# Two heads share a strip's weights in float32, and a final addition and a normalisation move behind the next maxima

## The chip, the cores and the metric

The kernel runs on one core of one Trainium2 chip. The metric is the time of one execution on the device in microseconds, as the median of several runs.

## The reference

Sixteen sequences of 256 tokens with 128 features go through three stages: `x += 0.5 * ffn(ln(x))`, `x += attn(ln(x))`, `x += 0.5 * ffn(ln(x))`. All is float32. `ffn` is a whole transformer block, `attn` a dilated attention whose queries, keys and values are the rows themselves.

```python
def ffn(x):                                  # 16 heads of 8 features, 8 experts, 2 chosen
    q, k, v = split(x @ w_qkv)
    scores = q @ k.T / sqrt(8)               # causal, 256 x 256 for each head
    h = layernorm(x + softmax(scores) @ v @ w_o) * g1 + b1
    w = two largest of softmax(h @ wg), normalised
    moe = sum over chosen e: w[e] * (gelu(h @ w1[e] + bb1[e]) @ w2[e] + bb2[e])
    return layernorm(h + moe) * g2 + b2
def attn(x):                                 # rate 4, segments of 64, so 4 interleaved sequences of 64
    return softmax(x @ x.T / sqrt(128)) @ x / 4
```

## The kernel before, in words

**Order.** A chunk is two sequences (512 tokens); eight chunks go through two passes of `ffn`, which makes 16 jobs `m`. The attention of one sequence is `n` (32 in all), and takes two *halves* of time. `make_order` (L53) writes one list by hand: for each half 17 slots (`SLOTS`, L48) in a fixed order, into which pieces of many stages are put. A half has `scores_0`, `first_c`, `turn_tiles`, `second_a`, `misc_1`, `exps_0`, `weigh_last`, `second_b`, `scores_1`, `misc_2`, `second_c`, `exps_1`, `weigh_0`, `first_a`, `misc_3`, `first_b`, `end`. Every engine walks through this one list and issues its own part of each piece, in this order, with semaphores between the engines. So an engine that waits in one piece holds back all its later pieces.

**Memory between the engines.** PSUM has eight banks: `ps_quad` of four, which scores and exponentials use in turn, in two pairs `a` (`pair_full`, `pair_free`), and `ps_ring` of four, which all other pieces take round robin (`take`, `full`, `freed`): a piece needs the bank that the piece four places earlier left.

**Attention of a job.** `norm`, `norm_apply`: layer norm on VectorE, with the power -0.5 on GpSimd (`powers`, L975). `turn`, `project` (L383): rows are transposed, queries and keys projected into `qk`, features on the partitions. `spread` (L312, SP's queue) writes `qk` to DRAM and reads it back with four DMAs so that heads lie in strips of 32 partitions: strip `i` of `q4` and `k4` holds, for group `j` of four, the 8 features of head `4j + i` at rows 4 to 11, and in rows 0 to 3 of `k4` constants (-1 in row `j`).
`scores(n, j)` (L398) does four heads, one in each strip: for each of the four a matmul over 256 keys for the later 128 queries (L409) and one over 128 keys for the earlier (L413), both with 32 rows and 128 columns of weights, then four full-array bf16 matmuls that add the causal mask (L417). VectorE takes row maxima over each pair of banks (L748), which frees the pair. After the fourth group `shift` transposes the maxima (L427), and VectorE adds them to the queries' unused rows (`q4s`, L765), so that the next product has them subtracted. `exps(n, j)` (L431) computes the scores again, keys as weights, per strip 128 queries (L439) and 256 queries (L443); ScalarE takes the exponential (L618), GpSimd zeroes what is above the diagonal (L972). `weigh` (L447) multiplies with the values, in column strips of 32. `rows`, `merge`, `attn_out` bring the result back. A float32 matmul stands in the profile as two instructions (two passes, each with its weight load).

**Behind it.** `mid_norm` and `mid_norm_apply` (L787, L791; L710 is the line of `normalise`, L1001 and L1004 are GpSimd's scale and offset), `turn_mid`, `route`, `gate`; per set of two jobs `rank` and `scatter` (rows sorted by expert, indirect DMAs L1017); 23 tiles in 8 batches through `turn_tiles`, `first` (L537), `second` (L546, whose output VectorE takes at L877), with a weight load from DRAM for each; `gather` (L1030), `combine`, `end_norm`, `end_norm_apply` (GpSimd's L1037) and `end_add` (VectorE's L910), which waits for L1037. `mid_norm_apply` and `end_add` stand in the slot `end`, directly ahead of the next half's `scores_0`. Between the passes the dilated attention `long_*` runs.

**Start.** VectorE fills `values`, `q4` and `k4` ahead of its first statistics; TensorE turns the bias (L583) once all small inputs and constants are there.

Of the kernel before, what the change touches and what calls it, by code (L numbers as in the profile page):

```python
# [25 lines left out]
SLOT = 32  # L26

# [22 lines left out]
FIRST_HALF, LAST_HALF = -9, HALVES + 25  # L50


def make_order():  # L53
# [18 lines left out]
    for m in range(JOBS):  # L72
        first = 4 * m
        put(first - 5, "misc_2", ("norm", m))
        put(first - 5, "misc_3", ("norm_apply", m))
        put(first - 4, "misc_1", ("turn", m))
        put(first - 4, "misc_2", ("project", m, 1))
        put(first - 4, "second_c", ("spread", m, 1))
        put(first - 4, "misc_3", ("project", m, 0))
        put(first - 4, "end", ("spread", m, 0))  # L80
        put(first - 1, "misc_1", ("values", m))
        put(first + 1, "misc_3", ("residual", m))
        put(first + 5, "misc_1", ("merge", m))
        put(first + 5, "misc_2", ("attn_out", m))
        put(first + 5, "misc_3", ("mid_norm", m))
        put(first + 5, "end", ("mid_norm_apply", m))
        put(first + 6, "misc_2", ("turn_mid", m))
        put(first + 6, "misc_3", ("route", m))
        put(first + 7, "misc_1", ("gate", m))

    for s in range(SETS):
# [17 lines left out]
        for c in range(2):  # L109
# [6 lines left out]
            put(first + 24 + c, "end", ("end_add", m))  # L116
            if m >= CHUNKS:
                put(first + 24 + c, "end", ("store", m - CHUNKS))
            else:
# [7 lines left out]
                put(half + 1, "end", ("long_values", m, 1))  # L127
    return [p for half in range(FIRST_HALF, LAST_HALF + 1) for slot in SLOTS for p in at[half, slot]]
# [10 lines left out]
def build(nc, x, w_qkv, w_o, g1, b1, wg, w1, bb1, w2, bb2, g2, b2, out):  # L139
# [8 lines left out]
    with ExitStack() as ctx:  # L148
# [9 lines left out]
        wqkv, wo, wgate = sb("wqkv", [P, 3 * D]), sb("wo", [P, D]), sb("wgate", [P, E])  # L158
        bb1_rows, bb1_t = sb("bb1_rows", [E * FC, P]), sb("bb1_t", [P, E * FC])
        g1_row, b1_row = sb("g1_row", [P, D]), sb("b1_row", [P, D])  # L160
        g2_row, b2_row = sb("g2_row", [P, D]), sb("b2_row", [P, D])
# [3 lines left out]
        row_of = sb("row_of", [P, SLOT])  # L165
# [3 lines left out]
        zeros = sb("zeros", [P, D])  # L169
# [5 lines left out]
        q4, k4 = sb("q4", [P, 2, GROUPS, TOK]), sb("k4", [P, 2, GROUPS, TOK])  # L175
        q4s = sb("q4s", [P, 2, GROUPS, S])
        values = sb("values", [P, 2, TT, HEADS, SLOT])
        probs = sb("probs", [P, PROBS, 4, 3 * P])
        part_max = sb("part_max", [P, 3, 4, GROUPS])
# [24 lines left out]
        weights = sb("weights", [P, WEIGHTS, ROW])  # L204
        act = sb("act", [P, ACTS, FC, P])
# [12 lines left out]
        small_in, x_in = sem("small_in"), sems("x_in", CHUNKS)  # L218
        const_dve, const_pool = sem("const_dve"), sem("const_pool")
# [9 lines left out]
        shift_ready, selected = sem("shift_ready"), sem("selected")  # L229
# [50 lines left out]
        CONSTANTS_DVE = 3  # L280
# [4 lines left out]
        def _(sp):  # L285
            sp.dma_start(xs[:, 0:TT, :], x_tiles[0]).then_inc(x_in[0], 16)
            sp.dma_start(wqkv[:, :], w_qkv).then_inc(small_in, 16)
            sp.dma_start(wo[:, :], w_o).then_inc(small_in, 16)
            sp.dma_start(wgate[:, :], wg).then_inc(small_in, 16)
            sp.dma_start(bb1_rows[:, :], bb1.rearrange("e (c p) -> (e c) p", p=P)).then_inc(small_in, 16)  # L290
            for row, given in ((g1_row, g1), (b1_row, b1), (g2_row, g2), (b2_row, b2)):
# [5 lines left out]
            def pack():  # L297
# [10 lines left out]
                for i in range(2):  # L308
                    sp.dma_start(sorted_h[i].rearrange("(t p) d -> p t d", p=P),
                                 zeros[:, :].unsqueeze(1).broadcast_to([P, TILES, D])).then_inc(zeroed, 16)  # L310

            def spread(m, which):  # L312
                rows = parts[m % 2, which]
                into = (q4, k4)[which]
                freed(sp, ("project", m, which))
                sp.dma_start(rows, qk[:, which, :]).then_inc(parts_out[which], 16)
                if m >= 2:
                    if which:
                        pair_used(sp, ("exps", 2 * m - 3, GROUPS - 1), 1)
                    else:  # L320
                        freed(sp, ("shift", 2 * m - 3))
                elif m == 0 and which:
                    sp.wait_ge(const_dve, CONSTANTS_DVE)
                    sp.wait_ge(const_pool, CONSTANTS_POOL)
                sp.wait_ge(parts_out[which], 16 * (m + 1))
                of_head = rows.rearrange("(j i d) t -> i d j t", j=GROUPS, i=4)
                for i in range(4):
                    sp.dma_start(into[32 * i + 4:32 * i + 4 + HD, m % 2, :, :], of_head[i]
                                 ).then_inc(parts_in[which][m % 2], 16)
# [12 lines left out]
            def load_weights(s, t):  # L342
                if t == 0:
                    sp.wait_ge(places_ready, s + 1)
                if (s, t) == (0, 0):
                    sp.wait_ge(packed_in, 16 * PACKED)
                k = tile_no(s, t)
# [13 lines left out]
            def store(c):  # L361
# [3 lines left out]
            pieces = {"spread": spread, "load_tiles": load_tiles, "load_weights": load_weights,  # L365
                      "store_tiles": store_tiles, "store": store}
            for kind, *at in ORDER:
                if kind in pieces:
                    pieces[kind](*at)
                if (kind, *at) == ("spread", 1, 0):  # L370
# [4 lines left out]
        def _(pe):  # L375
            def turn(m):
# [6 lines left out]
            def project(m, which):  # L383
# [3 lines left out]
                pe.matmul(bank(use), wqkv[:, which * D:(which + 1) * D], xn_t[:, :], start=True, stop=True  # L387
                          ).then_inc(ring_full, 1)

            def project_values(m):  # L390
                use = ("values", m)
                take(pe, use)
                for tt in range(TT):
                    mm = pe.matmul(bank(use)[:, tt * P:(tt + 1) * P], xn_t[:, tt * P:(tt + 1) * P],
                                   wqkv[:, 2 * D:3 * D], start=True, stop=True)
                mm.then_inc(ring_full, 1)

            def scores(n, j):  # L398
                m, at, par = n // 2, n % 2 * S, n // 2 % 2
                if j == 0 and n % 2 == 0:  # L400
                    for which in range(2):
                        pe.wait_ge(parts_in[which][par], 64 * (m // 2 + 1))
# [12 lines left out]
                for a in range(2):  # L415
                    for i in (2 * a, 2 * a + 1):
                        mm = pe.matmul(ps_quad[:, i, P:3 * P], ident_bf[:, :],  # L417
                                       causal[:, :].unsqueeze(1).broadcast_to([P, 2, P]), start=False, stop=True,
                                       skip_group_check=True)
# [11 lines left out]
            def exps(n, j):  # L431
                at, par = n % 2 * S, n // 2 % 2
                if j == 0:
                    freed(pe, ("shift", n))
                for a in range(2):
                    pe.wait_ge(pair_free[a], QUAD_NO["exps", n, j])
                    for i in (2 * a, 2 * a + 1):
                        rows = slice(32 * i, 32 * i + SLOT)
                        pe.matmul(ps_quad[:, i, 0:P], k4[rows, par, j, at + P:at + S], q4s[rows, n % 2, j, P:S],  # L439
                                  start=True, stop=True, tile_position=(32 * i, 0))  # L440
# [660 lines left out]
```

## Time and profile before

| | us |
|---|---|
| median of 3 runs | 1308.93 |
| lowest, highest | 1301.49, 1309.05 |
| the profiled execution | 1304.4 |
| its span, first to last instruction | 1302.6 |
| mean granted TensorE clock in it | 0.908 |

The profile is of one execution. The span is what views of the trace cover; 1.8 us of the execution lie outside it. "Idle before" is the time in which an engine had nothing running before an instruction, and the name behind it is what released it. The clock is given as a share of 2.4 GHz.

### The profile page before, as it was taken

The numbers are of one execution on the slowest core, as the hardware profiler recorded it, in microseconds if no ns is written. First come the engines' busy times: TensorE is split into PE (matmuls) and PEld (weight loads), VectorE is DVE, ScalarE is ACT, GpSimd is POOL, SyncE is SP. The second block draws the span as 40 slices with busy tenths as digits, with TensorE's granted clock in tenths as the row PEclk, the third lists the DMA queues.
The fourth block names the chain that finished last, engine by engine and source line by source line (L and its number), as shares of the span: only waits on it lengthen the run. The fifth ranks groups of instructions, "written<-read, shape, count | busy, mean of one in ns | idle before, by whom it ended". The sixth has DMA issues, their size and how long they took to land. (4 is left out here: it accounts for less than half of the span.)

```text
span 1302.6 us, 29447 instructions
## 1 busy us (share of the span) xinstructions
PE 1084.2 (83%) x11041; PEld 865.4 (66%) x11041; DVE 682.6 (52%) x2097; ACT 640.7 (49%) x1377; POOL 569.0 (44%) x708
## 2 busy tenths in 40 slices
PE   1788988899988898989989799988989799877570
PEld 0555655677776776867777577767777677776570
DVE  4445555545456664576555664566546654350313
ACT  0033333465656555645656466555546556633340
POOL 1023237222645446444645436454545436635505
PEclk8598888898989999989989899889989889988795
DMA  5085012463555435444545435363454445567661
GB/s 111 3 169 136 10 25 64 149 174 128 160 161 147 137 122 167 151 120 129 150 150 153 128 120 161 121 177 116 122 160 149 132 135 194 174 212 263 209 225 44
DMA packets 116467, 180.98 MB, mean 139 GB/s; under 512 B 12360, under 2 KB 79464, under 8 KB 116328
## 3 DMA queue, kind: packets, MB, share of 16 engines
q1 hardware_dynamic: 108136, 162.32, 43.2%
q0 software_dynamic: 8192, 16.79, 4.2%
q8 instruction: 89, 1.46, 0.5%
q14 instruction: 50, 0.41, 0.1%
HBM read 145.10 MB, written 38.68 MB: 141 GB/s over the span
## 5 line engine op out<-in xcount | busy, mean ns | idle before, releaser
L748 DVE TENSOR_REDUCE part_max<-ps_quad 128x6 f32<-128x768 f32 x256 | 233.1, 952 | 155.9 <-PE ps_quad L417 155.9
L618 ACT ACTIVATE probs<-ps_quad 128x768 f32<-128x768 f32 x256 | 196.0, 809 | 231.4 <-PE ps_quad L443 230.9
L972 POOL TENSOR_SCALAR_AFFINE_SELECT probs<-probs 128x512 f32<-128x512 f32 x256 | 162.2, 644 | 266.0 <-ACT probs L618 261.7
L654 ACT ACTIVATE act<-ps_ring,weights 128x128 f32<-128x128 f32 x736 | 205.3, 378 | 116.4 <-PE ps_ring L537 115.6
L537 PE MATMUL ps_ring<-tile_t,weights 128*128 128x128 f32 x1472 | 207.8, 288 | 23.1 <-DVE tile_y L877 12.9
L546 PE MATMUL ps_ring<-weights,act 128*128 128x128 f32 x1472 | 213.2, 294 | 9.0 <-DVE tile_y L877 5.4
L537 PEld LDWEIGHTS ps_ring<-tile_t,weights 128*128 128x128 f32 x1472 | 186.6, 199 | 39.8 <-issue 36.7
L546 PEld LDWEIGHTS ps_ring<-weights,act 128*128 128x128 f32 x1472 | 191.6, 204 | 30.0 <-issue 19.0
L977 POOL TENSOR_TENSOR rstd<-var_eps,power 128x4 f32<-128x4 f32 x56 | 57.9, 1034 | 275.4 <-DVE var_eps L704 275.4
L439 PE MATMUL ps_quad<-q4s,k 32*128 32x128 f32 x1024 | 100.5, 337 | 68.2 <-DVE part_max L748 68.2
L1030 POOL DMA_INDIRECT picked<-sorted_outputs,place x128 | 123.6, 966 | 76.5 <-issue 76.5
L877 DVE TENSOR_TENSOR tile_y<-ps_ring,weights 128x128 f32<-128x128 f32 x184 | 52.7, 287 | 187.8 <-PE ps_ring L546 187.6
L1017 POOL DMA_INDIRECT sorted_rows<-h_rows,place x128 | 124.3, 971 | 56.3 <-issue 33.9
L409 PE MATMUL ps_quad<-k,q 32*128 32x256 f32 x1024 | 123.2, 482 | 26.3 <-DMA q<-query_key_parts 21.3
L439 PEld LDWEIGHTS ps_quad<-q4s,k 32*128 32x128 f32 x1024 | 63.6, 194 | 104.5 <-issue 55.0
L443 PE MATMUL ps_quad<-q4s,k 32*128 32x256 f32 x1024 | 123.6, 403 | 0.0
L456 PE MATMUL ps_ring<-probs,values 128*32 128x256 f32 x1024 | 89.9, 426 | 3.2 <-POOL probs L972 2.7
L409 PEld LDWEIGHTS ps_quad<-k,q 32*128 32x128 f32 x1024 | 55.6, 209 | 51.9 <-DMA q<-query_key_parts 23.6
L417 PE MATMUL ps_quad<-causal,ident_bf 128*128 128x256 bf16 x512 | 83.5, 289 | 0.0
L413 PEld LDWEIGHTS ps_quad<-k,q 32*128 32x128 f32 x1024 | 72.5, 212 | 5.2
L654 ACT ACT_TABLE_LOAD x51 | 65.4, 1283 | 15.3 <-PE ps_ring L537 13.2
L413 PE MATMUL ps_quad<-k,q 32*128 32x128 f32 x1024 | 68.7, 294 | 0.0
(130 smaller groups left out, 1371.7 us busy)
## 6 DMA issues: line engine op xcount, KB each, us to landing
weights<-expert_weights SPq DMA_DIRECT2D x184, 578.0 KB, 4.9
tile_rows<-sorted_rows SPq DMA_DIRECT2D x56, 192.0 KB, 5.0
sorted_outputs<-tile_y SPq DMA_DIRECT2D x56, 192.0 KB, 2.2
query_key_parts<-qk SPq DMA_DIRECT2D x32, 256.0 KB, 2.0
k<-query_key_parts SPq DMA_DIRECT2D x64, 64.0 KB
q<-query_key_parts SPq DMA_DIRECT2D x64, 64.0 KB
sorted_rows<-zeros SPq DMA_DIRECT2D x2, 1472.0 KB, 10.8
xs<-in_L_attn_x SPq DMA_DIRECT2D x8, 256.0 KB, 6.7
```

The source lines that it names most:

```text
L409: pe.matmul(ps_quad[:, i, 0:S], q4[rows, par, j, at + P:at + S], k4[rows, par, j, at:at + S], start=True, stop=True, tile_position=(32 * i ...
L413: pe.matmul(ps_quad[:, i, S:3 * P], q4[rows, par, j, at:at + P], k4[rows, par, j, at:at + P], start=False, stop=True, tile_position=(32 * ...
L439: pe.matmul(ps_quad[:, i, 0:P], k4[rows, par, j, at + P:at + S], q4s[rows, n % 2, j, P:S], start=True, stop=True, tile_position=(32 * i, 0))
L443: mm = pe.matmul(ps_quad[:, i, P:3 * P], k4[rows, par, j, at:at + P], q4s[rows, n % 2, j, :], start=True, stop=True, tile_position=(32 * i ...
L537: mm = pe.matmul(bank(use)[:, f * P:(f + 1) * P], weights[:, k % WEIGHTS, f * P:(f + 1) * P], tile_t[:, n % 2, t % BATCH, :], start=True, ...
L546: mm = pe.matmul(bank(use)[:, 0:D], act[:, k % ACTS, f, :], weights[:, k % WEIGHTS, F + f * D:F + (f + 1) * D], start=(f == 0), stop=(f == ...
L618: sc.activation(probs[:, r % PROBS, 2 * a:2 * a + 2, :], ps_quad[:, 2 * a:2 * a + 2, 0:3 * P], ACT.Exp, scale=HD ** -0.5).then_inc(pair_fr ...
L654: ins = sc.activation(act[:, k % ACTS, f, :], bank(use)[:, f * P:(f + 1) * P], ACT.Gelu_apprx_tanh, bias=weights[:, k % WEIGHTS, 2 * F + f ...
L748: dve.tensor_reduce(part_max[:, :, heads, j].rearrange("p c i -> p i c"), ps_quad[:, heads, 0:3 * P].rearrange("p i (c k) -> p i c k", c=3 ...
L972: pool.affine_select(out=both, in_=both, compare_op=ALU.is_ge, fill=0.0, base=0, pattern=[[0, 2], [0, 2], [1, P]], channel_multiplier=-1). ...
L1017: pool.indirect_dma_start(sorted_h[s % 2][:, :], bass.IndirectOffsetOnAxis(place[:, s % 2, n * SET_TT + t:n * SET_TT + t + 1], 0), h_rows[ ...
L1030: pool.indirect_dma_start(picked[:, m % 2, n, tt, :], None, sorted_y[s % 2][:, :], bass.IndirectOffsetOnAxis(place[:, s % 2, n * SET_TT + ...
```

## The change

Layout: the 16 heads are spread as four strips with four heads each, in two groups `g` of two heads. Feature rows 4 to 19 of a strip hold both heads of a group. Where both heads are weights (`q_stack` for the scores, `k_stack` for the exponentials) they lie one above the other; the streamed side (`k_apart`, `q_apart`) has one column block for each head, with zeros in the other head's rows. The 16 columns' order of the weights for queries and keys is rearranged once (`w_qk`), so that the DMAs find the heads in place. A piece `(n, j)` still handles four heads, but in two strips, `2 * (j % 2)` and the next.

```diff
 def scores(n, j):
+    g, first = j // 2, j % 2 * 2
     for a in range(2):
         if no:
             pe.wait_ge(pair_free[a], no)
-        for i in (2 * a, 2 * a + 1):
-            rows = slice(32 * i, 32 * i + SLOT)
-            pe.matmul(ps_quad[:, i, 0:S], q4[rows, par, j, at + P:at + S], k4[rows, par, j, at:at + S],
-                      start=True, stop=True, tile_position=(32 * i, 0))
-        for i in (2 * a, 2 * a + 1):
-            rows = slice(32 * i, 32 * i + SLOT)
-            pe.matmul(ps_quad[:, i, S:3 * P], q4[rows, par, j, at:at + P], k4[rows, par, j, at:at + P],
-                      start=False, stop=True, tile_position=(32 * i, 0), skip_group_check=True)
+        rows = slice(SLOT * (first + a), SLOT * (first + a + 1))
+        pe.matmul(ps_quad[:, 2 * a, :], q_stack[rows, par, g, at + P:at + S],
+                  k_apart[rows, par, g, :, at:at + S].rearrange("r b (c k) -> r c b k", c=2),
+                  start=True, stop=True, tile_position=(SLOT * (first + a), 0))
+    for a in range(2):
+        rows = slice(SLOT * (first + a), SLOT * (first + a + 1))
+        pe.matmul(ps_quad[:, 2 * a + 1, 0:2 * P], q_stack[rows, par, g, at:at + P],
+                  k_apart[rows, par, g, :, at:at + P], start=True, stop=True,
+                  tile_position=(SLOT * (first + a), 0))
...
 def exps(n, j):
     if j == 0:
-        freed(pe, ("shift", n))
+        pe.wait_ge(q_ready, n + 1)
     for a in range(2):
         pe.wait_ge(pair_free[a], QUAD_NO["exps", n, j])
...
+        pe.matmul(ps_quad[:, 2 * a, :], k_stack[rows, par, g, at:at + P],
+                  q_apart[rows, n % 2, g, :, :].rearrange("r b (h q) -> r h b q", h=2),
+                  start=True, stop=True, tile_position=(SLOT * (first + a), 0))
+    for a in range(2):
+        rows = slice(SLOT * (first + a), SLOT * (first + a + 1))
+        pe.matmul(ps_quad[:, 2 * a + 1, 0:2 * P], k_stack[rows, par, g, at + P:at + S],
+                  q_apart[rows, n % 2, g, :, P:S], start=True, stop=True,
+                  tile_position=(SLOT * (first + a), 0)).then_inc(pair_full[a], 1)
```

The masks, the maxima, the exponentials, GpSimd's selection and `weigh` handle as many elements and columns as before, with other addresses. On VectorE `shift` becomes two steps:

```diff
-    dve.tensor_tensor(q4s[:, n % 2, :, :], q4[:, n // 2 % 2, :, n % 2 * S:n % 2 * S + S],
-                      bank(use)[:, 0:S].unsqueeze(1).broadcast_to([P, GROUPS, S]), ALU.add
+    dve.tensor_tensor(q_sum[:, :, :], q_stack[:, n // 2 % 2, :, n % 2 * S:n % 2 * S + S],
+                      bank(use)[:, 0:S].unsqueeze(1).broadcast_to([P, 2, S]), ALU.add
                       ).then_inc(free_sem(use), 1)
+    freed(dve, use)
+    dve.tensor_tensor(q_apart[:, n % 2, :, :, :], q_sum[:, :, :].unsqueeze(2).broadcast_to([P, 2, 2, S]),
+                      head_mask[:, :, :].unsqueeze(3).broadcast_to([P, 2, 2, S]), ALU.mult
+                      ).then_inc(q_ready, 1)
```

On SP's queue `spread` is parted into `spread_out` and `spread_in`, and the keys get eight DMAs more:

```diff
+for i in range(STRIPS):
+    at = SLOT * i + SHIFTS
+    sp.dma_start(into[at:at + STACK, m % 2, :, :], ...).then_inc(parts_in[which][m % 2], 16)
     if which:
+        for b in range(2):
+            given = SLOT * i + STACK * b
+            sp.dma_start(k_apart[at + HD * b:at + HD * (b + 1), m % 2, :, b, :], ...)
```

The order (`m` is a job, `first` its first half):

```diff
-        put(first - 4, "misc_1", ("turn", m))
-        put(first - 4, "misc_2", ("project", m, 1))
-        put(first - 4, "second_c", ("spread", m, 1))
-        put(first - 4, "misc_3", ("project", m, 0))
-        put(first - 4, "end", ("spread", m, 0))
+        put(first - 4, "turn_tiles", ("turn", m))
+        put(first - 4, "misc_1", ("project", m, 1))
+        put(first - 4, "second_b", ("project", m, 0), ("spread_out", m, 1))
+        put(first - 4, "misc_2", ("spread_out", m, 0))
+        put(first - 4, "second_c", ("spread_in", m, 1))
+        put(first - 4, "first_b", ("spread_in", m, 0))
...
-        put(first + 5, "end", ("mid_norm_apply", m))
-        put(first + 6, "misc_2", ("turn_mid", m))
-        put(first + 6, "misc_3", ("route", m))
+        put(first + 6, "first_c", ("mid_norm_apply", m))
+        put(first + 6, "misc_3", ("turn_mid", m))
+        put(first + 7, "turn_tiles", ("route", m))
...
-            put(first + 24 + c, "end", ("end_add", m))
+            put(first + 25 + c, "first_c", ("end_add", m))
```

Start: `values` is filled by GpSimd; VectorE fills the strips of one parity (`q_stack`, `k_apart`, `k_stack`: 1024, 2048 and 1024 elements a partition) and rearranges the weights of queries and keys, then goes to its first statistics; the other parity and the remaining constants come in a piece `constants` in half -5, and turning the bias becomes a piece `bias` in half -4. `w_qkv` is loaded in two parts with a semaphore of its own for the first. `zeros`, `bb1_rows` and the given weights lie in the expert weights' buffers, which are not used yet.

## Rows read from the trace of the kernel before

**Rows 1.** The page: busy us, share of the span and instructions by engine

```profile
PE 1084.2 (83%) x11041; PEld 865.4 (66%) x11041; DVE 682.6 (52%) x2097; ACT 640.7 (49%) x1377; POOL 569.0 (44%) x708
```

**Rows 2.** The table by stretches, each engine's busy us, then TensorE's clock

```profile
60.00:1125.00 1065.00, 956.49 (x10138) 751.33 (x10135) 600.95 (x1812) 578.53 (x1178) 488.77 (x572) 0.94 0.47 135
...
517.10:523.90 6.80, 6.80 (x52) 4.67 (x51) 0.33 (x2) 3.18 (x4) 2.13 (x3) 0.50 0.08 23
571.70:578.50 6.80, 6.80 (x51) 4.62 (x50) 4.92 (x20) 3.18 (x4) 2.33 (x3) 0.50 0.67 191
578.50:667.30 88.80, 79.05 (x856) 64.88 (x856) 55.23 (x171) 50.33 (x107) 44.22 (x50) 1.00 0.47 140
...
35.00:60.00 25.00, 20.18 (x134) 14.43 (x136) 13.54 (x27) 2.08 (x3) 1.61 (x2) 0.57 0.00 1
```

**Rows 3.** The waits: who waited for whom, us in total, times, longest

```profile
PE ps_quad L439 <- DVE part_max L748: 68.2, 33, 4.1
PE ps_quad L409 <- DMA q<-query_key_parts: 21.3, 5, 12.8
...
PE ps_ring L537 <- DVE tile_y L877: 12.9, 5, 6.1
```

**Rows 4.** The timeline of TensorE, one dense half (start us, us, what)

```profile
601.28 0.52 PE L439 MATMUL ps_quad<-q4s,k 32*128 32x128 f32 x8
601.60 0.63 PE L443 MATMUL ps_quad<-q4s,k 32*128 32x256 f32 x8
...
607.83 0.73 PE L409 MATMUL ps_quad<-k,q 32*128 32x256 f32 x8
608.37 0.41 PE L413 MATMUL ps_quad<-k,q 32*128 32x128 f32 x8
608.71 0.61 PE L417 MATMUL ps_quad<-causal,ident_bf 128*128 128x256 bf16 x4
```

**Rows 5.** The timeline of all engines at a stall, 565 to 573 us

```profile
569.33 0.69 DVE L910 TENSOR_TENSOR xs<-xs,end_rows 128x512 f32<-128x512 f32 x1 [5.52 <-POOL end_rows L1037]
...
570.95 0.49 PE L439 MATMUL ps_quad<-q4s,k 32*128 32x128 f32 x4 [4.10 <-DVE part_max L748]
571.16 0.31 PEld L443 LDWEIGHTS ps_quad<-q4s,k 32*128 32x128 f32 x4
571.27 0.63 PE L443 MATMUL ps_quad<-q4s,k 32*128 32x256 f32 x4
```

**Rows 6.** The timeline of TensorE, a matmul over 512 columns

```profile
554.79 1.02 PE L387 MATMUL ps_ring<-xn_t,wqkv 128*128 128x512 f32 x2
```

**Rows 7.** The timeline at the other stall, 659 to 668 us

```profile
659.38 1.22 DVE L765 TENSOR_TENSOR q4s<-q,ps_ring 128x1024 f32<-128x1024 f32 x1 [2.04 <-PE ps_ring L427]
...
663.16 2.06 DVE L710 TENSOR_SCALAR xn<-xn,moments,rstd 128x128 f32<-128x128 f32 x4 [1.16 <-POOL rstd L977]
...
666.24 0.49 PE L439 MATMUL ps_quad<-q4s,k 32*128 32x128 f32 x4 [3.25 <-DVE part_max L748]
```

**Rows 8.** The timeline of TensorE, the stall one set later

```profile
720.93 0.49 PE L439 MATMUL ps_quad<-q4s,k 32*128 32x128 f32 x4 [4.11 <-DVE part_max L748]
```

**Rows 9.** The groups by line: busy us, mean ns, idle before and releaser

```profile
L618 ACT ACTIVATE probs<-ps_quad 128x768 f32<-128x768 f32 x256 | 196.0, 809 | 231.4 <-PE ps_quad L443 230.9
...
L765 DVE TENSOR_TENSOR q4s<-q,ps_ring 128x1024 f32<-128x1024 f32 x32 | 39.1, 1220 | 33.0 <-PE ps_ring L427 30.5 <-DVE tile_y L877 2.5
```

**Rows 10.** The line of the inward DMAs on SP's queue

```profile
L328 SPq DMA_DIRECT2D k<-query_key_parts x64: 268/301/978, 23.9 to 1010.4; - x64
```

**Rows 11.** The timeline of the start, all engines

```profile
6.27 3.47 DVE L938 MEMSET q<- 128x4096 f32 x1 [0.80 <-issue]
...
10.61 2.78 DVE L951 TENSOR_SCALAR k<-row_of 128x512 f32<-128x512 f32 x8
...
13.53 0.28 PE L583 MATMUL ps_quad<-ident,bb_rows 32*128 32x32 f32 x1 [13.53 <-DVE k L951]
...
35.36 1.25 PE L409 MATMUL ps_quad<-k,q 32*128 32x256 f32 x8 [12.81 <-DMA q<-query_key_parts]
```

More of the change, by code:

```diff
@@ L26 @@
 SLOT = 32
+STRIPS = 4
+SHIFTS = HEADS // STRIPS
+STACK = 2 * HD
 JOBS = 2 * CHUNKS
@@ L115, in make_order @@
             put(first + 24 + c, "misc_3", ("end_norm_apply", m))
-            put(first + 24 + c, "end", ("end_add", m))
+            put(first + 25 + c, "first_c", ("end_add", m))
             if m >= CHUNKS:
-                put(first + 24 + c, "end", ("store", m - CHUNKS))
+                put(first + 25 + c, "first_c", ("store", m - CHUNKS))
             else:
@@ L127, in make_order @@
                 put(half + 1, "end", ("long_values", m, 1))
+    put(-5, "end", ("constants",))
+    put(-4, "misc_2", ("bias",))
     return [p for half in range(FIRST_HALF, LAST_HALF + 1) for slot in SLOTS for p in at[half, slot]]
@@ L309, in pack @@
                     sp.dma_start(sorted_h[i].rearrange("(t p) d -> p t d", p=P),
-                                 zeros[:, :].unsqueeze(1).broadcast_to([P, TILES, D])).then_inc(zeroed, 16)
-            def spread(m, which):
-                rows = parts[m % 2, which]
[L314 to L317, printed above, removed]
-                    if which:
[L319 to L329, printed above, removed]
+                                 zeros.unsqueeze(1).broadcast_to([P, TILES, D])).then_inc(zeroed, 16)
@@ L386, in project @@
                 take(pe, use)
-                pe.matmul(bank(use), wqkv[:, which * D:(which + 1) * D], xn_t[:, :], start=True, stop=True
+                pe.matmul(bank(use), w_qk[:, which, :], xn_t[:, :], start=True, stop=True
                           ).then_inc(ring_full, 1)
@@ L400, in scores @@
                 if j == 0 and n % 2 == 0:
-                    for which in range(2):
-                        pe.wait_ge(parts_in[which][par], 64 * (m // 2 + 1))
+                    pe.wait_ge(parts_in[0][par], 16 * STRIPS * (m // 2 + 1))
+                    pe.wait_ge(parts_in[1][par], 16 * 3 * STRIPS * (m // 2 + 1))
+                if n == 0 and j == 0:
+                    pe.wait_ge(bf_ready, 1)
                 no = QUAD_NO["scores", n, j]
+                g, first = j // 2, j % 2 * 2
                 for a in range(2):
@@ L451, in weigh @@
                     freed(pe, ("values", n // 2))
+                if n == 0 and j == 0:
+                    pe.wait_ge(values_set, 1)
                 pe.wait_ge(selected, 2 * EXP_NO["exps", n, j] + 2)
@@ L934, in long_values, with strips @@
                 ins.then_inc(free_sem(use), 1)
-            step(dve.memset(values[:, :, :, :, :], 0.0))
+            def strips(par):
+                dve.memset(q_stack[:, par, :, :], 0.0)
+                dve.memset(k_apart[:, par, :, :, :], 0.0)
+                dve.tensor_scalar(k_stack[:, par, :, :].rearrange("p g t -> p (g t)"),
+                                  shift_rows[:, :].broadcast_to([P, 2 * TOK]), -1.0, None, ALU.mult
+                                  ).then_inc(strips_set, 1)
@@ L953, in _ @@
-            ins.then_inc(const_dve, 1)
-            pieces = {"norm": norm, "norm_apply": norm_apply, "project": project, "values": project_values,
+            step(dve.tensor_reduce(shift_rows[:, :], row_of[:, 0:SHIFTS], AX.X, ALU.add))
+            settle()
+            strips(0)
+            dve.wait_ge(w_in, 16)
+            for which in range(2):
+                ins = dve.tensor_copy(w_qk[:, which, :].rearrange("p (r g) -> p r g", g=2),
+                                      w_given[:, which * D:(which + 1) * D].rearrange("p (g r) -> p r g", g=2))
@@ L956, in _ @@
+            ins.then_inc(weights_turned, 1)
+            pieces = {"constants": constants, "norm": norm, "norm_apply": norm_apply, "project":
+                      project, "values": project_values,
                       "scores": scores, "shift": shift, "rows": rows, "attn_out": attn_out, "mid_norm": mid_norm,
```

173 lines of the change are left out of this document (101 added, 72 removed).

## The prediction

> **What bounds the kernel now.** I read the page first: TensorE works 83% of the span, VectorE 52%, ScalarE 49%, GpSimd 44% [rows 1]. The table by stretches then gives what is to be worked with. From 60 to 1125 us, where attention runs, TensorE works 956.49 of 1065 us: 108.5 us are idle. Its mean granted clock there is 0.94; as it is either 2.4 or 1.2 GHz, about 0.06 x 2 x 1065 = 128 us pass at 1.2, in which 64 us of work are lost [rows 2]. So TensorE's stream of work sets the middle. Behind 1125 us neither scores nor exponentials are left; the change hardly touches that part. The waits say who makes the idle time: of all that TensorE waits for, 68.2 us in 33 waits (up to 4.1 us) stand on L439, the first exponential matmul, for VectorE's maxima L748; 21.3 us on the first scores, for queries and keys, 12.8 of them once at the start; the rest is small [rows 3].
>
> **Streaming in a strip.** Before, four heads lie in four strips and stream together. One scores piece in a dense place starts at 607.83, goes to the second group at 608.37 and to the masks at 608.71 [rows 4]. The 0.54 us are 0.11 of first weight load and 0.43 for both passes over 256 columns (1.7 ns a column); the 0.34 are 0.22 for 128 columns and 0.12 of gap before the full-array masks. Do four strips cost each other time? No: where only one pair of strips ran, the same L443 took 0.63 us for 4 instructions [rows 5], and with all four strips 0.63 us for 8 [rows 4]. The time goes by columns, not by strips.
> After, a piece has two matmuls over 512 columns in two strips at once, then two over 256. Two passes over 512 columns cost 0.86 us at that rate; L387, which has the shape, ends in 1.02 with its tail of 0.2 [rows 6]. So a scores piece streams 0.86 + 0.43 = 1.29 us where it was 0.43 + 0.22 = 0.65: +0.64. An exponential piece has the same column counts and loses the same 0.64. There are 32 jobs x 4 groups x 2 = 256 pieces: 256 x 0.64 = 164 us. Half of the weight loads go away, but all behind a piece's first lay beneath a streaming pass (0.31 of load beside 0.63 of matmul [rows 5]), and the first one stays: nothing gained. The four masks stay at 0.45.
> Bounds: if four strips did slow each other, 8 against 4 instructions of L439 (0.52 and 0.49) give 6%, and the loss is 256 x (0.64 - 0.08) = 143. Upwards, at the present mixture of clocks, 164 x 1.06 = 174. I take 164.
> The Trainium skill (TensorE: Matmul & The Clock Gate, Part 3 and its closing table) gives 3.07 times for four strips at 512 columns rather than four times. If two strips gave a full two times, a piece's 0.65 would become 0.65 x 3.07 / 2 = 1.00, the loss 256 x 0.35 = 89 us, and the time some 75 us below my sum, an estimate by that page. The rows with equal 0.63 us speak against it here.
>
> **The order on VectorE.** The final addition L910 and the middle normalisation stand now ahead of a half's first maxima. At 569.33 VectorE ends 5.52 us of waiting for GpSimd's L1037, adds (0.69) and only then reduces; TensorE starts L439 after 4.10 us idle [rows 5]. At 662 to 665 it is the four normalisations (2.06 us behind a wait of 1.16 for rstd), and 3.25 idle [rows 7]. Behind the maxima both have time: TensorE's next call on VectorE is for a bank of the ring of four, two or three pieces later, so about 3 us. The 33 waits go almost whole, but not where the reduction itself is late (some 0.8 us each in the early halves, about 10 us): -58, between -68 and -30.
> The clock comes with it. It was 1.2 GHz in 517.1 to 523.9 and in 571.7 to 578.5, each behind such a stall of 3 to 4 us, and 2.4 in the 88.8 us that follow [rows 2]. The pattern repeats every 150 us (the 4.10 us of 570.95 stand again, as 4.11, at 720.93 [rows 8]), so 7.1 times in 1065 us, with two low stretches of 6.8 us behind L439 stalls each time: 97 of the 128 us, 48 of lost work. I take -45, between -60 and 0. 0 is where other gaps keep it low.
>
> **Other edits.** VectorE: one addition of 1220 ns for 128x1024 becomes one over 128x512 (0.61 by the element, some 0.7 with its fixed part) and a multiplication over 1024 elements (at most 1.22): +0.7 us x 32 = 22 us on an engine 48% idle [rows 1, 9]. It lies between the shift and the next exponentials; there TensorE came 5.6 us after L765's end at 660.6 [rows 7]. Cover lost, it is those 22 us. Maxima, exponentials and masks handle as many elements as before: 0. Keys get 12 DMAs for 4, 0.30 us of issue each [rows 10]: 12 x 0.30 = 3.6 us of SP for 1.2, with queries, weight loads and tile loads queued behind. The keys are needed two halves on (some 35 us), and the outward copies now leave before the inward waits, so I take 0; uncovered, 16 x 2.4 = 38. The extra k_apart is 16 x 256 KB: 4 MB on 181, nothing. Route moves to the half of the rank; its 2 us of small VectorE steps may lengthen the existing rank stall: with the ring waits behind the moved pieces and the extra work at low clock I put +8 (0 to 30).
> Start: VectorE comes to its statistics at about 13.4, after two memsets of 3.47 (one of them the row's) and eight copies from 10.61 on (2.78); TensorE waits 13.53 for that and later 12.81 for queries [rows 11]. After, strips of one parity (0.87 + 1.74 + 0.7) and two small copies are ahead: 9 instead of 13.4, -4.4; copies out are sooner, the keys' issues later. -5 (-10 to +2).
>
> **The sum.** Span 1302.6 + 164 - 58 - 45 + 8 - 5 = 1366.6, and 1.8 more for the execution's own 1304.4: 1368. The median is 1308.93, 4.5 higher than the profiled one, and the three runs reach from 1301.49 to 1309.05, so I state 1370.
>
> **Rivals.**
> 1. Not slower, by idle time that takes up the cost. Place: the middle. If every one of the 108.5 idle us and of the 64 us of lost clock came back, 1304.4 + 164 - 172.5 - 5 = 1291. It decides where over 151 of these 172.5 are recovered. Against it: a third of the idle time is not at L439, and the exponentials' chain (maxima, then ScalarE's 0.81) grows too. Chance 0.04.
> 2. The clock does not come back. For it: from 35 to 60 us, where nearly only scores ran, the clock was 0.57 [rows 2], and strips are now half filled for twice as long. Against: there TensorE also sat idle between pieces. 1368 + 45 + 10 = 1423. Chance 0.13.
> 3. The waits move. VectorE still stands for L1037, now in front of the expert outputs L877 and the ring's fourth bank; half of the 58 returns and half of the clock with it: 1368 + 29 + 22 = 1419. For it: TensorE waits already at L537 for L877, 12.9 us in 5 waits [rows 3]. Chance 0.10.
> 4. The keys' twelve DMAs come late: 1368 + 38 = 1406. For it, 21.3 us of waits for queries exist. Against, most of it is the start. Chance 0.08.
> 5. Four strips did slow each other: 1368 - 21 = 1347 by the 6% of the L439 rows; this is the mechanism of the page named above. Chance 0.05.
> 6. The change does not do what it says: the pairs of strips don't overlap (each waits for its own bank). Then 1.29 more in each piece: 1304 + 2 x 164 and up, over 1550. The same-time rows of two strips exclude it nearly: 0.02.
> The forecast itself, 1335 to 1395: 0.58.
>
> **Numbers.** A measurement of this kernel tells about 1% from no change. Faster by over 1% (below 1296) is rival 1 at its full size: 0.03. Within 1% (to 1322): the rest of it and a bit of rival 5: 0.04. Slower 0.93. The range 1338 to 1412 holds the forecast, rivals 4 and 5 and the lower half of 2 and 3.
>
> **What would show it.** L409's successor with 4 instructions a piece, 512 columns, and about 1.5 us from its start to the masks (0.88 before). L439's successor without waits over 1.5 us for L748. Waits of TensorE for maxima below 15 us in all. Granted clock 0.97 or more from 250 us on. TensorE's busy time up by about 120 us (164 less what the clock gives). First scores at about 30 us instead of 35.36. It is wrong if a piece's two 512-column passes take much less than 0.86 us, if large waits appear at L877 or for keys, or if the clock falls.

## The result, and the profile after

The changed kernel takes 1422.8 us (1420.91 to 1428.16, four runs) beside 1308.46 for the kernel before: 1.089 times as long, with an interval of 1.085 to 1.094. The profiled execution has a span of 1420.7 us. Slower was forecast, but 1370 with an upper end of 1412. The direction was right; 61 us of growth was forecast and 114 came.

The page: busy times, then TensorE's slices and its clock in them.

```profile
PE 1276.5 (90%) x8993; PEld 873.0 (61%) x8993; DVE 690.0 (49%) x2129; ACT 635.9 (45%) x1377; POOL 579.0 (41%) x710
...
PE   2899999999999999999999999999999999877670
...
PEclk9756757657999999999999999999999999998895
```

TensorE is the wall more than before (90% for 83% [rows 1]). The clock's row shows where the loss lies: the second to the tenth slice stand at 5 to 7 tenths, and from the eleventh to the 36th there is only 9. The table by stretches of the kernel after: the first from the first masks (33.95 us) to those of the 33rd piece of scores, the second to those of the last piece, the third the rest, and one stretch out of the first. The columns are TensorE, its weight loads, VectorE, ScalarE and GpSimd, busy us and instructions, then the clock.

```profile
34.00:320.00 286.00, 268.98 (x1242) 135.70 (x1241) 112.05 (x268) 58.65 (x96) 66.66 (x85) 0.66 0.24 64
320.00:1210.00 890.00, 865.85 (x6700) 612.87 (x6701) 499.05 (x1552) 496.10 (x1041) 414.77 (x469) 0.98 0.46 139
1210.00:1421.00 211.00, 133.68 (x1037) 121.09 (x1034) 67.58 (x279) 78.04 (x234) 90.33 (x93) 0.83 0.58 185
51.60:109.60 58.00, 54.37 (x196) 24.00 (x196) 18.17 (x35) 10.63 (x16) 8.63 (x12) 0.50 0.67 147
```

The same three stretches of the kernel before:

```profile
37.00:232.50 195.50, 165.72 (x1722) 111.71 (x1719) 108.56 (x267) 60.75 (x96) 67.41 (x87) 0.86 0.32 74
232.50:1095.00 862.50, 782.30 (x8226) 630.69 (x8226) 493.15 (x1522) 498.29 (x1041) 406.63 (x468) 0.94 0.49 144
1095.00:1303.00 208.00, 129.61 (x1079) 119.62 (x1075) 66.95 (x278) 78.50 (x234) 90.49 (x93) 0.83 0.59 187
```

In 51.6 to 109.6 us TensorE worked 54.37 of 58 us, with no pause over 0.8 us, and all of it at 1.2 GHz. That is the new thing. The fall itself is not new. The kernel before has it at the same place, behind the same wait for the shift's columns, and there it lasts 10.2 us:

```profile
52.14 0.45 PE L427 MATMUL ps_ring<-ident,shift_cols 128*128 128x128 f32 x2 [2.07 <-DVE shift_cols L758]
...
52.90:63.10 10.20, 9.06 (x61) 6.29 (x54) 5.30 (x13) 2.11 (x3) 2.29 (x3) 0.50 0.00 1
```

In the kernel after, the wait is as long, and the clock is back only at 109.6, behind the masks and eight full-array instructions of L501:

```profile
51.90 0.69 PE L452 MATMUL ps_ring<-ident,shift_cols 128*128 128x128 f32 x2 [2.06 <-DVE shift_cols L790]
...
107.08 1.03 PE L443 MATMUL ps_quad<-causal,ident_bf 128*128 128x256 bf16 x4
107.91 1.86 PE L501 MATMUL ps_ring<-ident,attn_t 128*128 128x128 f32 x8
```

From 48 to 322 us the clock falls six times: at 51.6, 167.6, 246.1 and 321.2 in waits of 2.04 to 2.27 us for VectorE's maxima and shift, at 123.2 and 270.0 behind gaps of 0.83 and 0.61 us. It comes back each time at the end of an unbroken run of full-array work: the masks and then L501 or L520 (attention's way out), the last time the expert tiles (L567). From 55.38 to 60.04 there was full-array work too, with a pause of 0.75 us in it, and the clock stayed low.

The 118 us of longer span part as follows. At mean clock c a stretch of t us has 2(1 - c)t us at 1.2 GHz, and half of that is lost.

| | first 32 pieces | other 96 | outside |
|---|---|---|---|
| length before, after | 195.5, 286 | 862.5, 890 | 244.6, 244.7 |
| streaming, 1.22 us a piece of both kinds (2 x 0.61, rows below) | +39 | +117 | |
| lost to the clock, before, after | 27, 97: +70 | 52, 18: -34 | |
| TensorE idle, before, after | 29.8, 17.0: -13 | 80.2, 24.2: -56 | |
| sum (difference) | +96 (+90.5) | +27 (+27.5) | 0 |

The waits of TensorE, us in total, times, longest:

```profile
PE ps_quad L464 <- DVE part_max L780: 17.1, 22, 2.3
...
PE ps_quad L433 <- DMA q_stack<-query_key_parts: 12.4, 1, 12.4
PE ps_ring L567 <- DVE tile_y L913: 12.2, 5, 5.9
```

L464, which is L439's successor, waits 17.1 us where it was 68.2 [rows 3]. From 322 to 1210 us TensorE waits nowhere longer than 1.3 us for VectorE; before, the longest were 4.1.

TensorE's timeline in the dense part, one scores piece and one exponential piece:

```profile
700.36 1.13 PE L433 MATMUL ps_quad<-k_apart,q_stack 32*128 32x512 f32 x4
701.32 0.60 PE L438 MATMUL ps_quad<-k_apart,q_stack 32*128 32x256 f32 x4
701.85 0.61 PE L443 MATMUL ps_quad<-causal,ident_bf 128*128 128x256 bf16 x4
...
705.02 1.13 PE L464 MATMUL ps_quad<-q_apart,k_stack 32*128 32x512 f32 x4
705.98 0.60 PE L469 MATMUL ps_quad<-q_apart,k_stack 32*128 32x256 f32 x4
706.51 0.64 PE L484 MATMUL ps_ring<-probs,values 128*32 128x256 f32 x8
```

From 700.36 to the masks at 701.85 it is 1.49 us, where it was 0.88 [rows 4], and from 705.02 to 706.51 again 1.49: +0.61 a piece. 1.52 was the forecast (0.11 + 1.29 + 0.12), +0.64. An early scores piece in the same view:

```profile
64.91 2.08 PE L433 MATMUL ps_quad<-k_apart,q_stack 32*128 32x512 f32 x4
...
67.77 1.03 PE L443 MATMUL ps_quad<-causal,ident_bf 128*128 128x256 bf16 x4
```

64.91 to 67.77: 2.86 us, the same work at half the clock.

The groups of both new steps of the shift (busy, mean ns, idle before):

```profile
L801 DVE TENSOR_TENSOR q_apart<-q_sum,head_mask 128x1024 f32<-128x1024 f32 x32 | 41.1, 1283 | 1.1
...
L797 DVE TENSOR_TENSOR q_sum<-q_stack,ps_ring 128x512 f32<-128x512 f32 x32 | 22.0, 688 | 50.4 <-PE ps_ring L452 49.1 <-DVE tile_y L913 1.3
```

688 + 1283 ns for 1220 [rows 9]: +0.75 us each, as reckoned.

### The profile page after: what moved, and what is told of

Its sections match the earlier page's. It is cut to its first block and busy times, and to the rows that moved or that the text cites. A ratio compares the mean times of both kernels' runs of the same rounds, so it can differ in the third digit from the quotient of the medians.

```text
span 1420.7 us, 25520 instructions
## 1 busy us (share of the span) xinstructions
PE 1276.5 (90%) x8993; PEld 873.0 (61%) x8993; DVE 690.0 (49%) x2129; ACT 635.9 (45%) x1377; POOL 579.0 (41%) x710
## 5 line engine op out<-in xcount | busy, mean ns | idle before, releaser
L567 PE MATMUL ps_ring<-tile_t,weights 128*128 128x128 f32 x1472 | 206.7, 289 | 21.2 <-DVE tile_y L913 12.2
L464 PE MATMUL ps_quad<-q_apart,k_stack 32*128 32x512 f32 x512 | 196.4, 711 | 17.1 <-DVE part_max L780 17.1
L576 PE MATMUL ps_ring<-weights,act 128*128 128x128 f32 x1472 | 202.8, 285 | 7.7 <-DVE tile_y L913 4.2
L567 PEld LDWEIGHTS ps_ring<-tile_t,weights 128*128 128x128 f32 x1472 | 186.6, 201 | 34.3 <-issue 32.7
L433 PE MATMUL ps_quad<-k_apart,q_stack 32*128 32x512 f32 x512 | 188.1, 728 | 19.3 <-DMA q_stack<-query_key_parts 12.4
L576 PEld LDWEIGHTS ps_ring<-weights,act 128*128 128x128 f32 x1472 | 185.3, 198 | 23.3 <-issue 18.2
L1072 POOL DMA_INDIRECT sorted_rows<-h_rows,place x128 | 128.2, 1002 | 50.7 <-issue 34.0
L469 PE MATMUL ps_quad<-q_apart,k_stack 32*128 32x256 f32 x512 | 114.6, 412 | 0.0
L469 PEld LDWEIGHTS ps_quad<-q_apart,k_stack 32*128 32x128 f32 x512 | 70.5, 206 | 67.1 <-issue 64.7
L438 PEld LDWEIGHTS ps_quad<-k_apart,q_stack 32*128 32x128 f32 x512 | 69.5, 210 | 65.5 <-issue 61.4
L438 PE MATMUL ps_quad<-k_apart,q_stack 32*128 32x256 f32 x512 | 106.2, 418 | 0.0
L464 PEld LDWEIGHTS ps_quad<-q_apart,k_stack 32*128 32x128 f32 x512 | 57.7, 200 | 68.5 <-issue 32.3
L433 PEld LDWEIGHTS ps_quad<-k_apart,q_stack 32*128 32x128 f32 x512 | 54.8, 207 | 57.8 <-issue 25.5
L443 PE MATMUL ps_quad<-causal,ident_bf 128*128 128x256 bf16 x512 | 87.4, 299 | 0.0
```

Of the source, the lines that this page charges most:

```text
L433: pe.matmul(ps_quad[:, 2 * a, :], q_stack[rows, par, g, at + P:at + S], k_apart[rows, par, g, :, at:at + S].rearrange("r b (c k) -> r c b ...
L438: pe.matmul(ps_quad[:, 2 * a + 1, 0:2 * P], q_stack[rows, par, g, at:at + P], k_apart[rows, par, g, :, at:at + P], start=True, stop=True, ...
L464: pe.matmul(ps_quad[:, 2 * a, :], k_stack[rows, par, g, at:at + P], q_apart[rows, n % 2, g, :, :].rearrange("r b (h q) -> r h b q", h=2), ...
L469: pe.matmul(ps_quad[:, 2 * a + 1, 0:2 * P], k_stack[rows, par, g, at + P:at + S], q_apart[rows, n % 2, g, :, P:S], start=True, stop=True, ...
L567: mm = pe.matmul(bank(use)[:, f * P:(f + 1) * P], weights[:, k % WEIGHTS, f * P:(f + 1) * P], tile_t[:, n % 2, t % BATCH, :], start=True, ...
L576: mm = pe.matmul(bank(use)[:, 0:D], act[:, k % ACTS, f, :], weights[:, k % WEIGHTS, F + f * D:F + (f + 1) * D], start=(f == 0), stop=(f == ...
```

## The experiments

The theory after the result, called A: two strips in flight stream for twice as long, and they don't bring the clock back once it has fallen; the dense part has enough full-array work between, the early part has not. The rivals: the clock stays low for gaps (B), or for the zeros among the streamed rows, or the layout's own steps cost the time. These kernels ran on other chips than the first comparison; the kernel before takes about 1387 us there, so ratios to the kernel before on the same chip are compared.

**Strips by themselves.** Behind the last piece of the kernel before, matmuls are appended that nothing reads.

```diff
+def two_strips(rounds):
+    for _ in range(rounds):
+        for i in range(2):
+            rows = slice(32 * i, 32 * i + SLOT)
+            pe.matmul(ps_quad[:, i, :], q4[rows, 0, 0, 0:P], k4[rows, 0, 0, :], start=True, stop=True,
+                      tile_position=(32 * i, 0))
...
+full_array(12)
+four_strips(35)
+two_strips(35)
+one_strip(35)
+two_strips(35)
+four_strips(35)
+full_array(12)
+two_strips(35)
+full_array(12)
...
```

> The kernel before, with nine stretches of matmuls that feed nothing appended behind TensorE's last piece: float32, 128 columns of weights, 512 streamed, 35 rounds each (12 for the full array): full array, four strips, two strips, one strip, two strips, four strips, full array, two strips, full array; then alternating two strips and full array. TensorE never waits in them. Theory A (the clock follows how much of the array streams): 2.4 GHz is held with four strips and with the full array, and is lost within the two-strip or the one-strip stretch and not regained while only two strips stream, so a round of two strips (0.86 us at 2.4 GHz) becomes 1.71 us; four strips regain it. Theory B (the clock follows whether TensorE has work, and fell in the early halves for the gaps there): all stretches at 2.4 GHz, 0.86 us a round with one, two or four strips. The time itself grows by the stretches, some 300 to 450 us.

The table by stretches; one after the other four strips, two, one, two, four, full array, two:

```profile
1390.00:1420.00 30.00, 30.00 (x280) 14.32 (x282) 0.00 (x0) 0.00 (x0) 0.00 (x0) 1.00 0.01 2
1420.00:1450.00 30.00, 30.00 (x144) 13.41 (x139) 0.00 (x0) 0.00 (x0) 0.00 (x0) 1.00 0.00 1
1452.50:1505.00 52.50, 52.50 (x63) 20.17 (x62) 0.00 (x0) 0.00 (x0) 0.00 (x0) 0.50 0.00 0
1507.00:1565.00 58.00, 58.00 (x138) 28.14 (x136) 0.00 (x0) 0.00 (x0) 0.00 (x0) 0.50 0.00 0
1569.00:1597.00 28.00, 28.00 (x264) 16.00 (x258) 0.00 (x0) 0.00 (x0) 0.00 (x0) 1.00 0.00 1
1598.00:1639.00 41.00, 41.00 (x97) 18.12 (x96) 0.00 (x0) 0.00 (x0) 0.00 (x0) 1.00 0.00 0
1639.50:1669.00 29.50, 29.50 (x138) 13.19 (x140) 0.00 (x0) 0.00 (x0) 0.00 (x0) 1.00 0.00 1
```

Four strips and two strips behind them ran 30 us each at 2.4 GHz. One strip streams from 1450.07 on; at 1452.5 the clock fell, and it stayed low. The two strips that came next streamed for 58 us without a gap at 1.2 GHz, 4 instructions in 1.7 us; the four strips after them began at about 1566.4 and were at 2.4 from 1568.6 on. Theory A was wrong in one half, that two strips lose the clock: behind a fast stretch they hold it (also at 1639.5). They only don't raise it. Theory B has fallen: TensorE never paused in these 58 us. The full array never started from a low clock here; behind the last row it and two strips went on in turns to 1900 us, all at 2.4. A round of two or four strips costs the same 0.86 us at 2.4 GHz, and a round of one strip 1.67 us at 1.2 GHz, as one of two strips does there (1.7).

**The moves alone**, in the kernel before:

```diff
-        put(first + 5, "end", ("mid_norm_apply", m))
-        put(first + 6, "misc_2", ("turn_mid", m))
-        put(first + 6, "misc_3", ("route", m))
+        put(first + 6, "first_c", ("mid_norm_apply", m))
+        put(first + 6, "misc_3", ("turn_mid", m))
+        put(first + 7, "turn_tiles", ("route", m))
...
-            put(first + 24 + c, "end", ("end_add", m))
+            put(first + 25 + c, "first_c", ("end_add", m))
```

> The kernel before with its four strips, and of the change only the places of middle normalisation, final addition, turn_mid, route and store. Theory A: the waits of L439's kind fall from 68 us to under 20, and the low clock stretches behind them go too: 1302.6 - 50 - 40, so 1205 to 1240 us in all. Rival (waits only move to the expert outputs or to GpSimd's scaling): 1285 to 1310 us, with new waits of TensorE for L877's successor.

0.949 times before (0.944 to 0.955): of 1308 us 66 less, so 1242, just above what was expected. Its waits:

```profile
PE ps_quad L409 <- ACT probs L618: 16.7, 21, 1.6
...
PE ps_quad L439 <- DVE part_max L748: 15.5, 24, 2.3
```

15.5 us for 68.2. The place of the final addition [rows 5], in this kernel:

```profile
568.87 1.82 DVE L748 TENSOR_REDUCE part_max<-ps_quad 128x6 f32<-128x768 f32 x2 [2.69 <-remote]
...
569.88 0.49 PE L439 MATMUL ps_quad<-q4s,k 32*128 32x128 f32 x4 [0.69 <-DVE part_max L748]
...
570.61 0.68 DVE L910 TENSOR_TENSOR xs<-xs,end_rows 128x512 f32<-128x512 f32 x1
```

VectorE reduces at once, TensorE waits 0.69 us instead of 4.10, and the addition follows at 570.61, when GpSimd has its rows ready. Other waits grew a little (the scores wait 16.7 us for ScalarE's exponentials, 3.7 in the kernel before), which may be why the gain falls short of waits and clock added up; as the two ran on different chips, that is not shown.

**Each move by itself.**

> The kernel before with only the middle normalisation behind the maxima (and turn_mid and route later, as in the change). Of the three waits of 4.1, 2.5 and 3.4 us in a set of 150 us two hold a middle normalisation: if waits simply add up, this gives half to two thirds of the 5.1% of both moves, 0.966 to 0.975 times before. If they hang together (the final addition alone keeps the wait), under 1%.

> The kernel before with only the final addition (and the store) behind the maxima: if the waits add up, the rest of the 5.1%: 0.974 to 0.985 times before, with the wait of 4.1 us at the place of 570 us gone and that of 3.4 us at 666 us still there.

The normalisation alone: 0.968 (0.966 to 0.970). The addition alone: 0.989 (0.986 to 0.994), less than the 0.974 to 0.985 expected. The two add to 4.3% where both together give 5.1%, so they about add up within the intervals. What TensorE still waits for the maxima, with the normalisation alone and then with the addition alone:

```profile
PE ps_quad L439 <- DVE part_max L748: 29.6, 26, 3.7
```

```profile
PE ps_quad L439 <- DVE part_max L748: 59.7, 36, 5.5
```

Of 68.2 us of these waits the normalisation takes 38.6 and the addition 8.5; both together take 52.7.

**The new strips without the moves.**

> The changed kernel with the five moved places (middle normalisation, final addition, turn_mid, route, store) put back to where they stood before. Theory A: the dense part loses what the moves gave, some 55 us of waits and 40 us of clock; the early part stays slow: 1422.8 + 95, so 1480 to 1530 us. Rival (longer streaming alone gives VectorE the time, so that the moves bring nothing here): 1420 to 1445 us.

**The change once more**, for a chip in common with the other experiments:

> The changed kernel itself, once more, so that it stands beside the other kernels of this call on one chip. Nothing is changed. 1.089 times the kernel before, within 1%.

1.155 (1.147 to 1.163) without the moves, 1.075 (1.070 to 1.080) with them; the latter is over a point below the first chip's 1.089, just outside what was written. Waits, then the stretch 60 to 1125, without the moves:

```profile
PE ps_quad L464 <- DVE part_max L780: 78.6, 28, 5.5
```

```profile
60.00:1125.00 1065.00, 972.49 (x6266) 628.44 (x6265) 486.46 (x1445) 434.63 (x888) 375.10 (x437) 0.82 0.36 105
```

And the change itself, its waits and stretches:

```profile
PE ps_quad L464 <- DVE part_max L780: 17.8, 19, 2.3
```

```profile
60.00:250.00 190.00, 178.68 (x829) 88.47 (x832) 68.56 (x157) 42.10 (x69) 37.30 (x51) 0.64 0.26 62
60.00:1125.00 1065.00, 1011.71 (x6850) 663.40 (x6849) 521.99 (x1567) 476.28 (x970) 414.17 (x478) 0.87 0.38 114
```

The rival, that longer streaming makes the moves idle, falls: they give 6.9% here, more than in the kernel before. 78.6 us of waits become 17.8, and the clock goes from 0.82 to 0.87. One place shows what may lie behind it: without the moves TensorE waits 3.87 us for the maxima up to 669.29, and 13.6 us at 1.2 GHz follow (668.4 to 682.0), where the kernel before had 6.8 behind each of the two stalls of [rows 2].

**One head from each of four strips**, with the rest of the change kept, zeros and DMAs included:

```diff
-    rows = slice(SLOT * (first + a), SLOT * (first + a + 1))
-    pe.matmul(ps_quad[:, 2 * a, :], q_stack[rows, par, g, at + P:at + S],
-              k_apart[rows, par, g, :, at:at + S].rearrange("r b (c k) -> r c b k", c=2), ...)
+    for i in (2 * a, 2 * a + 1):
+        rows = slice(32 * i, 32 * i + SLOT)
+        pe.matmul(ps_quad[:, i, 0:S], q_stack[rows, par, g, at + P:at + S],
+                  k_apart[rows, par, g, head, at:at + S], ...)
```

> The changed kernel with its whole layout (both heads as weights in a strip, zeros on the streamed side, 12 key DMAs, two steps of the shift, all moves, the new start), but a piece takes one head of each of the four strips instead of both heads of two: 256 and 128 columns in four strips. Theory A (the cost is that two strips stream twice as long, and the clock that falls with them): 164 us of streaming and about 100 us of low clock in the early part go, 1422.8 - 190 to 215, so 1205 to 1240 us, near the kernel with the moves only. Rival (layout, masking multiplication, DMAs or zeros cost the time or the clock): over 1300 us, and the clock under 0.8 in 60 to 250 us.

0.957 (0.953 to 0.960), 1325.7 us where the change takes 1489.5 on a chip with the same time for the kernel before: 164 us less. In the first chip's time that is 1252, 12 above the theory's range and far under the rival's 1300. The table by stretches:

```profile
60.00:250.00 190.00, 157.22 (x1658) 103.26 (x1659) 104.17 (x269) 60.48 (x97) 70.99 (x88) 0.87 0.36 93
250.00:1125.00 875.00, 805.62 (x8384) 649.55 (x8376) 506.74 (x1628) 511.72 (x1074) 425.90 (x477) 0.96 0.48 146
```

The clock is 0.87 early, beside 0.64 in the change. Zeros, masking multiplication and the keys' twelve DMAs are all in here, so they neither bring down the clock nor cost much: against the moves alone it is 0.7%, where the intervals touch.

**Four strips in the first eight sequences only**, a quarter of the pieces. Below the first line stands one head from each of four strips, below the second the change's own form:

```diff
+    if n < EARLY:
+        ...
+    else:
         ...
```

> The changed kernel, but its first eight sequences (32 of 128 pieces of scores and as many of exponentials, a quarter) take one head of each of four strips, the rest both heads of two strips as in the change. Theory A (the early part pays twice, for longer streaming and for a clock that two strips do not raise again; the dense part only for streaming, half of it out of waits): 32 x 1.28 = 41 us of streaming and about 50 us of lost clock go, so 80 to 100 us less than the changed kernel, over half of the whole cost for a quarter of the pieces: 1.02 to 1.03 times before. Rival (the cost is streaming alone and lies evenly): a quarter of 171 us, 43 us less: 1.055 to 1.06 times before.

1.014 (1.010 to 1.018), 1407.3 us in the middle of three runs (a fourth took 1427.9), where the change takes 1489.5: 82 us less, where an even share was 43 and the theory said 80 to 100. (The ratio written down lay higher as it began from 1.089.) The stretches:

```profile
60.00:250.00 190.00, 154.96 (x1617) 100.95 (x1617) 103.81 (x263) 59.87 (x95) 70.50 (x86) 0.87 0.37 95
250.00:1125.00 875.00, 833.61 (x6276) 586.99 (x6273) 471.47 (x1475) 463.04 (x972) 383.43 (x436) 0.96 0.44 133
```

The early clock is 0.87 again, and the 33rd piece's masks stand at 242.4 us, in the change at 319.1: 77 of the 82 us. A quarter of the pieces carries half of the cost.

**Filling the idle strips** in the first ten sequences, between the 512-column and the 256-column matmuls:

```diff
+for a in range(2):
+    strip = (first + 2) % 4 + a
+    idle = slice(SLOT * strip, SLOT * strip + SLOT)
+    mm = pe.matmul(ps_quad[:, 2 * a + 1, 0:FILL], held[idle, :], streamed[idle, :],
+                   start=True, stop=True, tile_position=(SLOT * strip, 0))
+mm.then_inc(filled, 1)
...
+pe.wait_ge(filled, filled_no[0])
```

> The changed kernel plus work that nothing reads: in the first ten sequences' pieces, while two strips stream 512 columns, the two idle strips stream 384 columns of the same tiles, into the two banks that the piece overwrites afterwards; TensorE then waits for the end of that before the 256-column matmuls. Theory A: the clock comes back in the early part (above 0.9 from 60 to 250 us instead of 0.64), and the kernel gets faster by added work: 1330 to 1370 us. Theory B, or a clock that falls for the zeros or for gaps: 1420 to 1445 us, with the clock as before.

1.065 (1.059 to 1.071): three runs of 1469.2 to 1486.7 us and a fourth, the profiled one, of 1491.8. The middle of the three is 1474.9, 15 below the change's 1489.5. The change stands at 1.075 (1.070 to 1.080); the intervals touch, and it ran on another chip with the same time for the kernel before, so the whole time shows no sure gain. The stretch 60 to 250:

```profile
60.00:250.00 190.00, 173.23 (x1071) 74.07 (x1072) 74.08 (x166) 44.26 (x74) 40.54 (x55) 0.87 0.26 62
```

The clock did come back, 0.87 for 0.64, by nothing but more work in the array. From the first masks to those of the 41st piece, where the fill ends, first in this kernel and then in the change:

```profile
34.00:385.00 351.00, 319.41 (x2061) 152.34 (x2057) 145.71 (x359) 95.11 (x176) 82.39 (x106) 0.90 0.27 73
```

```profile
34.00:396.40 362.40, 342.98 (x1759) 186.26 (x1757) 144.81 (x359) 97.00 (x176) 82.66 (x106) 0.70 0.26 71
```

By the formula above the low clock costs 35 us here and 109 in the change, 74 less, but the part is only 11 us shorter. 1330 to 1370 us was expected, in the first chip's time it is 1393: the price of the added work was not reckoned. TensorE's timeline, a scores piece in the early part:

```profile
141.61 0.70 PE L449 MATMUL ps_quad<-k_apart,q_stack 32*128 32x512 f32 x2
141.62 0.91 PE L430 MATMUL ps_quad<-k_apart,q_stack 32*128 32x384 f32 x4
...
142.84 0.70 PE L455 MATMUL ps_quad<-k_apart,q_stack 32*128 32x256 f32 x4
143.47 0.61 PE L460 MATMUL ps_quad<-causal,ident_bf 128*128 128x256 bf16 x4
```

141.61 to 143.47 are 1.86 us to the masks where the dense piece of the change has 1.49: the fill starts behind the second pair's matmul, and the 256 columns wait for its end. In 80 pieces that would be 30 us, an estimate from this one; TensorE also stood idle 31.6 us for 19.4. The rest of the 63 us that the fill cost is not explained.

## Why the prediction was wrong

**What held.** The streaming: 1.49 us a piece for a forecast 1.52, so 256 x 0.61 = 156 for 164 us. That two strips and four differ by 164 us in the experiment, the very sum, is luck: clock and absorbed waits are in it. The waits: those for the maxima fell from 68.2 to 17.1, so 51 for a forecast 58, with 2.3 as the longest where none over 1.5 was forecast; all idle time fell by 13 + 56 = 69. VectorE's two steps (+0.75 for +0.7), the keys' DMAs (no wait but the first, 12.4 us), and the start (L433 at 31.09 for 35.36 before, -4.3 for -5).

**The step that failed** is "The clock comes with it: -45". In the dense part it was right: 34 us came back, and long runs at 2.4 GHz stand in the place of the low stretches. In the first 32 pieces it went the other way, +70. Together +36 for -45 is 81 us on the wrong side, more than the 53 by which the forecast missed. Idle time that fell by 69 for 58 took back 11, streaming 8; the +8 for the pieces moved and the -5 of the start, 3 together, came out as 0 outside the two parts, and some 5 are not assigned. TensorE's busy time grew by 192 us where about 120 was to show the forecast right. The wait at 52 us that lowers the clock is the same before and after (2.07 and 2.06 us); what differs is how long the clock stays down behind it, 10.2 us and 58. The error lay in treating the clock as a matter of gaps alone. The row that spoke against it was on the table: 0.57 in 35 to 60 us, where scores ran nearly alone [rows 2]. It stood there as an argument of rival 2 and was put aside for the pauses in it. The repetition every 150 us was read from the dense part and spread over the whole middle, though the early part has other work.

**The rivals.** Rival 2 gave 1423 us at a chance of 0.13, and the time is 1422.8, but not for its reason: it had the clock stay as it was everywhere, while it rose late and fell early. Rival 1 (not slower) had the right mechanism, idle time that takes up the cost, and in the dense part it nearly came true: 117 us of streaming cost 27.5. Rivals 3 and 4 did not come. Rival 5 is excluded: in the appended stretches four strips take the same 0.86 us a round as two, and one as long as two, so four are four times as much as one. The four-strip figure of the Trainium skill (TensorE: Matmul & The Clock Gate, Part 3), 3.07 times, does not hold in these stretches. The same page of the Trainium skill ties the clock to how busy TensorE is (Part 1). By the row of 51.6 to 109.6, busy at 1.2 GHz, that alone does not decide.

**Open.** It was not tried where between two strips and the full array a mixture begins to raise the clock; why the full-array work from 55.38 to 60.04, with one short pause, did not raise it is not explained. Removing the wait of 2.06 us at 51.9, to see whether the early clock then holds, was not tried either. Nor is it known why the kernel before takes 6% longer on the chips of the experiments. The changed kernel keeps step on both up to the 41st piece's masks (396.7 and 396.4 us) and falls behind only after that.

## What to carry to other kernels

Count small matmuls by the strips in flight, not by instructions or weight loads: fewer, longer matmuls in half of the strips cost twice the time here (1.29 for 0.65 us of streaming by the forecast, +0.61 measured). When a change empties part of the array, split the kernel by what else TensorE does there and forecast the clock for each part; a stretch that the old profile shows slow in spite of work is a warning. And the cheap half of this change, VectorE's maxima first and the pieces that wait for GpSimd after, is worth 5% by itself: the kernel before with only the moves, at 0.949, beats both.

## What was unexpected of the hardware

- The clock has memory. Two strips streaming without a pause held 2.4 GHz for 30 us behind four strips, and stayed at 1.2 for 58 us behind one strip; four strips brought it back after about 2.2 us.
- Behind the same wait of 2.1 us it stayed low for 10.2 us with four strips in flight, and for 58 us with two.
- TensorE's busy share does not tell the clock: 94% busy at 0.50 in 51.6 to 109.6 us.
- Added work can raise the clock: idle strips filled with matmuls that nothing reads took the early part from 0.64 to 0.87, and of 74 us of clock 11 were left as gain there.
